# A transformer block on one core: last expert tiles planned in three segments, first keys ahead of other heads, ranks set anew

## The chip, the cores and the metric

The kernel runs on one core of a Trainium2 chip. Its time is the device time of one execution in microseconds (us). Beside it there is one profiled execution, with its own time and its own span (from the first to the last instruction). Engines: PE (TensorE, matrix products), DVE (VectorE), ACT (ScalarE), POOL (GpSimd), SP (SyncE, which here only issues transfers).

## The reference, cut to what matters

x is 4 batches of 512 tokens with 256 channels. Four layers follow each other, each added to x after a layer norm:

```python
x = x + _L0_attn_a_ref(_layernorm(x, axis=-1), ...)   # causal attention, 16 heads of 16, 4 key groups
x = x + _L0_ffn_ref(_layernorm(x, axis=-1), ...)      # 8 experts, the best 2 per token, 256 -> 176 -> 256
x = x + _L0_attn_b_ref(_layernorm(x, axis=-1), ...)   # memory attention, 4 banks of memories
x = x + _L0_ffn_ref(_layernorm(x, axis=-1), ...)      # the same experts again
```

The expert layer is `silu(x Wg) * (x Wu)`, times Wd, weighted by the two router probabilities. It is float32; the first attention is float16 with float32 sums.

## The kernel before

**The order is planned.** Each piece of work is a step with an engine, a rank, an assumed time and the steps it needs (`Work.add`, L122). `Work.order` (L141) goes through them as a list scheduler: it takes the step that can start first by the assumed times, or one of lower rank on the same engine that can start within PATIENCE times the first one's time. `NUDGE` (L94) adds a number to the rank of a kind of step. The result is a fixed order for each engine, and each engine executes its steps in it; a wait stops all that stands behind. `after` means that the step before must have finished (with `lands`, its transfer has landed), `behind` only that it was issued. In the first microseconds PE is given "warm" products where it would be idle (`keep_warm`, L130).

**The head.** SP issues x of batch 0 in two halves, the constants (`first_pack`), then the rest of x and the late constants (`load_late`). Then come the norm, the transposes (`f_turn`), q, k and v, and for the keys and queries the cosines, sines, mean square, `inv_rms`, `rotate`, in two parts p: 0 holds the queries of the first four heads and all keys, 1 the other heads. `first_keysT` and `place_keys` put group 0's keys into `kbd`, ACT two copies and DVE two (L1224, L1462). Scores run in 11 units per group and batch: `first` gives the maxima (PE L1002, DVE L1477), `second` the probabilities (PE L1025, ACT L1303), then `values`.

**Experts.** A token's normalised row is scattered twice (POOL, L1861) into a region of `xs` per expert. Within an expert the rows lie in the order batch, tile, token. 39 tiles of 128 rows (`TILES`) are worked through per layer: `load` (SP L903, 8 buffers), `xT` (PE L1119), `gate_up` (PE L1138, ACT L1347, DVE L1685 and L1689), `hidden` (PE L1147), `down` (PE L1155, DVE L1698 into `yo`, POOL L1876 scatters the rows into `ys`, 4 buffers). Which tile belongs to which expert and where its rows start is worked out by DVE (`plan`, L1575 to 1663) in three stages: 9 tiles as soon as 2 batches are routed, 8 with the third, 22 with the last. In the last stage there are SEGS = 16 segments, first what is left of each expert's full or mixed tiles of batches 0 to 2, then each expert's tiles that need batch 3. So tiles below MIXED = 31 hold all rows of the first three batches. Before the last stage SP writes zero rows behind each expert's rows (`pads`, L884), then it loads.

**Memory attention.** Per batch: `mq`, `den` (PE L1165, L1176), and per tile of 128 tokens `main` (PE L1184, DVE L1724, POOL L1883), `combT` (PE L1193: the sum of two banks' halves, transposed), `mem_out` (PE L1201, DVE L1740).

**The end.** `combine` (L455): for a batch of the second expert layer SP fetches `ys` in two halves of two transfers each (`fetch`, L913), DVE adds them to x (`join`, L1734 and L1735), SP stores each half (`store`, L919). Batches 0 to 2 wait for tile 30, batch 3 for tile 38. There are two fetch buffers in `kbd`, so a fetch waits for the join two batches before it.

## Time and profile before

| | before |
|---|---|
| median of 3 runs | 534.54 us (533.55 to 538.16) |
| the profiled execution | 532.43 us |
| its span | 530.6 us |
| granted clock over the span | 0.979 |
| PE busy | 480.4 us (91%) |
| DVE, ACT, POOL busy | 374.0 (70%), 269.3 (51%), 248.3 (47%) |
| HBM read and written | 28.89 and 25.00 MB |

How to read it: busy time counts an engine's instructions; matrix products are pipelined and their ends are modelled, so PE at 91% is not PE at its peak. The granted clock is a share of TensorE's 2.4 GHz; 0.50 is its lower level. A row of the timeline gives the start, the time, the engine, the line, the operation with what it writes and reads, and in square brackets how long the engine had been idle before and what released it. SPq and POOLq are issuing times of transfers. In the chain that ended last, each piece is what released the next.

### The profile page before, as it was taken

Reading aid. Unit: us, or ns where it says so; the run is one execution under the profiler, and the core shown is the slowest. Engines: PE = TensorE matmul, PEld = TensorE weight load, DVE = VectorE, ACT = ScalarE, POOL = GpSimd, SP = SyncE. Lnnn points to the kernel's source line nnn. Section 1 sums busy time; section 2 is a strip of 40 time slices with the busy share of each in tenths; the row PEclk is TensorE's granted clock in tenths of the full one; section 3 lists DMA queues with packets and bytes.
Section 4 is the critical chain, followed back from the end, with each engine's and each line's share of the span. In section 5 each row is a group of like instructions: output and inputs, shape, how many; then the busy total and the mean of one; then the engine's idle time right before and its main releaser. Section 6 shows DMA issues by size and latency. Waiting matters only on the chain.

```text
span 530.6 us, 10938 instructions
## 1 busy us (share of the span) xinstructions
PE 480.4 (91%) x3364; PEld 326.9 (62%) x3364; DVE 374.0 (70%) x1098; ACT 269.3 (51%) x642; POOL 248.3 (47%) x308
## 2 busy tenths in 40 slices
PE   7798999999999999899999979999979998999960
PEld 3445655765765676676676646675747765677740
DVE  5999989889999866754445557867878675344563
ACT  4587898887887874333333416514133533343310
POOL 5419339238650162473424654446464746333330
PEclk9899999999999999999999999999999989999995
DMA  8363800111230432374335492112141446433485
GB/s 276 129 261 142 178 19 10 53 58 45 62 101 2 121 111 71 115 196 136 105 101 168 81 179 40 41 40 81 40 141 60 149 132 181 130 100 117 148 279 182
DMA packets 43736, 60.77 MB, mean 115 GB/s; under 512 B 5856, under 2 KB 38240, under 8 KB 43040
## 3 DMA queue, kind: packets, MB, share of 16 engines
q1 hardware_dynamic: 33696, 38.24, 24.0%
q0 software_dynamic: 9984, 21.83, 13.9%
q8 instruction: 29, 0.48, 0.4%
q14 instruction: 27, 0.22, 0.1%
HBM read 28.89 MB, written 25.00 MB: 102 GB/s over the span
## 4 chain that ended last, share of the span: by engine, by line
PE 53%; DVE 12%; issue 5%; DMA 5%; POOL 4%; ACT 3%; SPq 1%; POOLq 0%; DVEq 0%; ACTq 0%
PE PS L1138 13%; PE PS L1155 9%; PE PS L1025 4%; PE PS L1184 3%; PE PS L1002 3%; POOL xs L1861 3%; PE PS L1119 2%; PE PS L1087 2%; PE PS L1147 2%; DMA ys<-yo,xin 2%; PE PS L1193 2%; DVE smax L1477 2%; PE PS L1201 2%; DMA kbd<-ys 2%; PE PS L1076 2%
## 5 line engine op out<-in xcount | busy, mean ns | idle before, releaser
L1876 POOL DMA_INDIRECT ys<-yo,xin x78 | 75.3, 966 | 106.2 <-DVE yo L1698 96.9
L1138 PE MATMUL PS<-wexp,xTt 128*128 x312 | 106.1, 467 | 2.7 <-issue 1.6
L1477 DVE TENSOR_REDUCE smax<-PS 128x1 f32<-128x512 f32 (+3 forms) x176 | 102.3, 634 | 6.6 <-PE PS L1004 6.1
L1303 ACT ACTIVATE prob<-PS 128x512 f16<-128x512 f32 (+1 forms) x176 | 92.7, 562 | 20.5 <-PE PS L1027 19.2
L1861 POOL DMA_INDIRECT xs<-xn,pos x64 | 62.5, 976 | 58.8 <-DVE pos L1572 41.7
L1155 PE MATMUL PS<-wexp,hT 88*128 x312 | 81.2, 387 | 2.3 <-ACT hT L1353 2.1
L1138 PEld LDWEIGHTS PS<-wexp,xTt 128*128 128x128 f32 x312 | 55.4, 191 | 25.3 <-issue 5.5
L1347 ACT ACTIVATE th<-PS 128x176 f32<-128x176 f32 x78 | 24.7, 317 | 84.0 <-PE PS L1138 84.0
L1685 DVE SCALAR_TENSOR_TENSOR sg<-th,PS 128x176 f32<-128x176 f32 x78 | 26.2, 336 | 58.2 <-ACT th L1347 57.9
L1155 PEld LDWEIGHTS PS<-wexp,hT 88*128 88x128 f32 x312 | 55.8, 191 | 15.2 <-issue 4.2
L1025 PE MATMUL PS<-qT,kbd 128*128 128x512 f16 (+3 forms) x256 | 60.8, 299 | 2.3 <-ACT qT L1295 1.0
L1002 PE MATMUL PS<-kbd,qT 128*128 128x512 f16 (+1 forms) x176 | 59.1, 360 | 2.7 <-DVE smax L1477 1.7
L1698 DVE TENSOR_SCALAR yo<-PS,xin 128x256 f32<-128x256 f32 x78 | 37.4, 482 | 27.8 <-PE PS L1155 22.1
L1353 ACT ACTIVATE hT<-PS 88x256 f32<-88x256 f32 x78 | 29.6, 379 | 41.4 <-PE PS L1147 40.4
L1027 PE MATMUL PS<-ident_b,mask_b 128*128 128x128 bf16 (+2 forms) x176 | 42.7, 243 | 0.0
L1004 PE MATMUL PS<-mask_b,ident_b 128*128 128x128 bf16 (+2 forms) x176 | 42.7, 243 | 0.0
L1043 PEld LDWEIGHTS PS<-vaug,prob 128*128 128x128 f16 x640 | 32.8, 96 | 16.0 <-ACT prob L1303 2.7
L1043 PE MATMUL PS<-vaug,prob 128*128 128x17 f16 x640 | 38.5, 171 | 1.5 <-ACT prob L1303 1.3
L1184 PE MATMUL PS<-late_rows,qT 128*128 128x512 f32 x64 | 32.2, 604 | 5.1 <-DVE qa L1724 4.7
L1147 PE MATMUL PS<-first_rows,hf 128*88 128x128 f32 x156 | 30.2, 275 | 4.8 <-DVE hf L1689 4.5
L1883 POOL TENSOR_TENSOR qa<-qa 128x256 f32<-128x256 f32 x32 | 23.2, 756 | 22.7 <-DVE qa L1724 22.6
L1025 PEld LDWEIGHTS PS<-qT,kbd 128*128 128x128 f16 x256 | 21.4, 98 | 15.8 <-ACT prob L1303 3.6
(210 smaller groups left out, 842.3 us busy)
## 6 DMA issues: line engine op xcount, KB each, us to landing
xin<-xs SPq DMA_DIRECT2D x78, 129.0 KB, 2.1
kbd<-ys SPq DMA_DIRECT2D x20, 256.0 KB, 4.1
wexp<-in_experts SPq DMA_DIRECT2D x4, 1216.0 KB, 9.2
xs<-zeros SPq DMA_DIRECT2D x32, 129.0 KB, 4.0
xn<-xn SPq DMA_DIRECT2D x8, 512.0 KB, 3.3
xall<-ys POOLq DMA_DIRECT2D x6, 512.0 KB, 7.2
out<-xall SPq DMA_DIRECT2D x8, 256.0 KB, 2.7
kbd<-kT SPq DMA_DIRECT2D x60, 32.0 KB, 2.2
```

Source lines behind the costliest of these rows:

```text
L1002: pe.matmul(o, qT1[:, b % 2, g, i * P:(i + 1) * P], kbd[:, g, r0:r0 + nr, 0:w], start=True, stop=False, skip_group_check=True)
L1004: pe.matmul(o[:, :, i * P:w], ident_b[:], mask_b[:].unsqueeze(1).to_broadcast([P, nr, P]), start=False, stop=True, skip_group_check=True). ...
L1025: pe.matmul(o[:, k], kbd[:, g, r0 + k, j * P:(j + 1) * P], qT2[:, g % 2, j * P:S], start=(k == 0), stop=False, skip_group_check=True)
L1027: pe.matmul(o[:, :, 0:P], mask_b[:], ident_b[:].unsqueeze(1).to_broadcast([P, nr, P]), start=False, stop=True, skip_group_check=True).then ...
L1043: mm = pe.matmul(o[:, i, r0 + k], prob[:, u % NPR, k * w + (i - j) * P:k * w + (i - j + 1) * P], vaug[:, b, j, g], start=(n == 0 and k == ...
L1138: mm = pe.matmul(PS[:, bank, 0:2 * FI], xTt[:, j % NXT, kc * P:(kc + 1) * P], wexp[:, bass.ds(expert[f, j], 1), kc * 2 * FI:(kc + 1) * 2 * FI]
L1155: mm = pe.matmul(PS[:, bank, 0:D], hT[:, j % 2, c * P:(c + 1) * P], wexp[0:FH, bass.ds(expert[f, j], 1), DOWN + c * D:DOWN + (c + 1) * D] ...
L1184: pe.matmul(PS[:, bank], sig[:, b % 2, kc, i * P:(i + 1) * P], late["mem"][:, kc], start=True, stop=True).then_inc(filled[bank], 1)
L1303: act.activation(prob[:, u % NPR, 0:nr * w], PS[:, bank, 0:nr * w], ACT.Exp, scale=ATT_SCALE)\
L1477: dve.tensor_reduce(smax[:, i, REP * g + r0:REP * g + r0 + nr], PS[:, bank, 0:nr * w].rearrange("p (r w) -> p r w", r=nr), AX.X, ALU.max). ...
L1861: pool.indirect_dma_start(xs[f], bass.IndirectOffsetOnAxis(pos[:, f, b, i, k:k + 1], axis=0), xn[:, b % 2, i, k], None).then_inc(scattered ...
L1876: pool.indirect_dma_start(ys[f], bass.IndirectOffsetOnAxis(xin[:, j % NXIN, D + 1:D + 2].bitcast(I32), axis=0), yo[:, j % NYO], None).then ...
```

## The change

- **Three parts.** SEGS is 24. In the last stage, batch 3's tiles are in two parts: what its first 256 tokens need, then the rest. Tiles below MIXED_HALF = 35 hold all rows of that first half, and `fetch` of half 0 of batch 3 waits for tiles 31 to 34. In the planner the second half's fetch stands `behind` the first one's, no longer `after` it. `count` on PE gives a second set of counts (5 small products more). DVE's final plan works on 24 segments; the mask and the table `upto` are bfloat16, and the table is made by DVE in `bank_shift` (two operations) in place of being loaded.
- **First keys.** DVE's cosines and mean square of the other heads stand behind its `place_keys`, and that behind the first queries. ACT places one copy of the keys, DVE three.
- **Loads and presets.** SP waits for the constants before it issues `load_late`. The memset of `kbd` is four of a quarter each.
- **combT** is a transpose and a product that adds to it, in place of two products.
- **The planner:** NUDGE is new throughout, PATIENCE is 0.13 for 0.022, some assumed times differ, and after 10 us the warm products stand closer (0.16 for 0.25) until 24.

The diff, cut to its core (of NUDGE, the first lines):

```diff
 MIXED = 2 * (B - 1) * S // P + NE - 1
-SEGS = 2 * NE
+MIXED_HALF = (2 * (B - 1) * S + S) // P + NE - 1
+SEGS = 3 * NE
 PLAN_N = [-(-(hi - lo) // 4) * 4 for _, lo, hi in STAGES]
...
-NUDGE = {("apply", 0): 4.5, ("bank_shift",): -3, ("combT", 2): 0.5, ("combT", 3): -18, ("cosines", 1): 12,
...
-         ("xT", 0): 54, ("xT", 1): 1}
+NUDGE = {("bank_shift",): 3, ("banks",): 17, ("combT", 1): 19, ("combT", 2): -21, ("count", 0): -17,
+         ("den", 2): 7, ("f_stats", 2): -31, ("first", 0): 16, ("first", 1): 25, ("first", 3): 2,
+         ("gate_up", 0): 2, ("gate_up", 1): 2, ("hidden", 0): -10, ("inv_rms", 1): 14, ("join", 1): 73,
+         ("load_x", 0): 11, ("main", 0): -2, ("main", 1): -10, ("main", 2): 37, ("main", 3): -9,
...
-    WARM_FROM, WARM_UNTIL, WARM_GAP, WARM_STEP = 3.2, 25.0, 0.4, 0.25
-    HOP, PATIENCE = 0.05, 0.022
+    WARM_FROM, WARM_RISE, WARM_UNTIL, WARM_GAP, WARM_STEP = 3.2, 10.0, 24.0, 0.4, (0.25, 0.16)
...
-def tiles_with(b):
-    return MIXED if b < B - 1 else TILES
+def tiles_with(b, h=1):
+    return MIXED if b < B - 1 else TILES if h else MIXED_HALF
...
     for p in range(2):
+        ahead = [(DVE, "place_keys")] if b == 0 and p else []
         last = [(p0, "queries", b - 1, p)] if b else []
         w.add(POOL, r(), (1.75, 2.05)[p], "sines", b, p, after=made + [(POOL, "constants")] + last)
-        w.add(e, r(), ((0.75, 0.95), (1.3, 1.75))[b > 0][p], "cosines", b, p, after=made + [(POOL, "constants")] + last)
+        w.add(e, r(), ((0.75, 0.95), (1.3, 1.75))[b > 0][p], "cosines", b, p, after=made + [(POOL, "constants")] + last, behind=ahead)
         w.add(ACTE, r(), (0.53, 0.75)[p], "square", b, p, after=made + [(p0, "mean_square", b - 1, p)] * (b > 0))
-        w.add(e, r(), ((0.85, 1.1), (2.2, 2.7))[b > 0][p], "mean_square", b, p, after=[(ACTE, "square", b, p)])
+        w.add(e, r(), ((0.85, 1.1), (2.2, 2.7))[b > 0][p], "mean_square", b, p, after=[(ACTE, "square", b, p)], behind=ahead)
         w.add(ACTE, r(), 0.45, "inv_rms", b, p, after=[(e, "mean_square", b, p)] + last)
         w.add(e, r(), ((0.65, 0.92), (1.55, 2.1))[b > 0][p], "rotate", b, p, after=[(POOL, "sines", b, p), (e, "cosines", b, p)])
...
-                for a in (ACTE, DVE):
-                    w.add(a, r(), 1.0, "place_keys", after=[(PE, "keysT" if a == ACTE else "first_keysT", *[b] * (a == ACTE)),
-                                                            (POOL, "presets")])
+                place_rank = r()
+                w.add(ACTE, place_rank, 0.5, "place_keys", after=[(PE, "keysT", b), (POOL, "presets")])
         w.add(e, r(), ((0.38, 0.95), (0.6, 1.75))[b > 0][p], "queries", b, p, after=[(ACTE, "inv_rms", b, p), (e, "rotate", b, p),
               (e, "keys", b), (DVE, "presets")] + old + [(e, "queries", b, 0)] * p)
         if p == 0:
             w.add(ACTE, r(), 0.5, "keysT", b, after=[(PE, "keysT", b)] + [(ACTE, "place_keys")] * (b == 0)
                   + [(SP, "place_keys", b - 2, g) for g in range(b == 2, NG) if b >= 2])
+            if b == 0:
+                w.add(DVE, place_rank, 1.27, "place_keys", after=[(PE, "first_keysT"), (POOL, "presets")],
+                      behind=[(DVE, "queries", 0, 0)])
             for g in range(b == 0, NG):
                 w.add(SP, r(), 2.4, "place_keys", b, g, after=[(ACTE, "keysT", b), (POOL, "presets")] + [(PE, "second", b - 1, g, NU - 1)] * (b > 0),
...
-    w.add(PE, rank, 0.1, "count", f, n, after=[(DVE, "choose", f, b) for b in range(STAGES[n][0])], banks=banks,
+    w.add(PE, rank, 0.3 if n == LAST else 0.1, "count", f, n, after=[(DVE, "choose", f, b) for b in range(STAGES[n][0])], banks=banks,
           emptied=(DVE, "plan", f, n, 3 if n == 1 else 0))
-    prior = [(DVE, "plan", f, n - 1, 3)] if n else [(DVE, "down", f - 1, TILES - 1)] if f else [(DVE, "presets")]
-    for part, time in enumerate((1.67, 1.9 if n == LAST else 1.3, 1.1 if n == LAST else 0.85, 1.5)[:4 - (n == LAST)]):
+    prior = [(DVE, "plan", f, n - 1, 3)] if n else [(DVE, "down", f - 1, TILES - 1)] if f else [(DVE, "bank_shift")]
+    for part, time in enumerate((2.9 if n == LAST else 1.67, 2.9 if n == LAST else 1.3, 1.6 if n == LAST else 0.85, 1.5)[:4 - (n == LAST)]):
         w.add(DVE, rank, time, "plan", f, n, part, after=[(DVE, "plan", f, n, part - 1)] if part else
               [(PE, "count", f, n)] + prior)
...
-    done = tiles_with(b)
-    rows = [(POOL, "down", f, j) for j in range(done - NYO, done)]
+    rows = [[(POOL, "down", f, j) for j in range(tiles_with(b, h) - NYO, tiles_with(b, h))] for h in range(2)]
     n = JOINED.index((f, b)) if (f, b) in JOINED else None
     for k in range(2):
         if n is None:
-            w.add(POOL, rank + 0.1 * k, 1.4, "add", f, b, k, after=rows + [(POOL, "add", f, b, 0)] * k,
+            w.add(POOL, rank + 0.1 * k, 1.4, "add", f, b, k, after=rows[1] + [(POOL, "add", f, b, 0)] * k,
                   behind=[(POOL, "pow", 1, 0)], lands=8.0)
         else:
-            w.add(SP, rank + 0.1 * k, 0.75, "fetch", f, b, k, after=rows + ([(DVE, "join", *JOINED[n - 2], 1)] if n >= 2 else [])
-                  + [(SP, "fetch", f, b, 0)] * k, lands=3.3)
+            w.add(SP, rank + 0.1 * k, 0.75, "fetch", f, b, k, after=rows[k] + ([(DVE, "join", *JOINED[n - 2], 1)] if n >= 2 else []),
+                  behind=[(SP, "fetch", f, b, 0)] * k, lands=3.3)
     for h in range(2 * (n is not None)):
...
                   behind=prior(DVE))
             w.add(POOL, times[i], 0.7, "main", b, i, kc, after=[(DVE, "main", b, i, kc)], behind=prior(POOL))
...
-        w.add(PE, times[i + 1], 0.89, "combT", b, i, after=[(POOL, "main", b, i, kc) for kc in range(KC)], banks=(3, 4),
+        w.add(PE, times[i + 1], 0.66, "combT", b, i, after=[(POOL, "main", b, i, kc) for kc in range(KC)], banks=(3, 4),
...
     w.add(SP, -998, 0.5, "load_x", 1, behind=[(SP, "load_x", 0)], lands=2.8)
-    w.add(SP, -997, 0.5, "constants", behind=[(SP, "load_x", 1)], lands=6.3)
-    w.add(SP, -996, 4.0, "load_late", behind=[(SP, "constants")], lands=11.0)
+    w.add(SP, -997, 0.5, "constants", behind=[(SP, "load_x", 1)], lands=5.0)
+    w.add(SP, -996, 4.0, "load_late", after=[(SP, "constants")], lands=10.0)
     w.add(SP, unit(2), 2.0, "load_experts", behind=[(SP, "place_keys", 0, NG - 1)], lands=20.0)
...
+        pl_mask = sb("pl_mask", [P, JL, SEGS], BF16)
+        upto = sb("upto", [P, SEGS, SEGS], BF16)
         pl_prod = sb("pl_prod", [P, JL, SEGS])
         pl_base = sb("pl_base", [P, JL])
...
                     elif kind == "load_late":
+                        sp.wait_ge(first_loaded, 16)
...
                     elif kind == "fetch":
                         f, b, h = a
-                        for j in range(tiles_with(b) - NYO, tiles_with(b)):
+                        for j in range(tiles_with(b, h) - NYO, tiles_with(b, h)):
                             wait_for_row(sp, f, j)
                         n = JOINED.index((f, b))
                         if n >= 2:
...
                                            stop=(c == batches - 1))
+                        if batches == B:
+                            for c in range(B - 1):
+                                pe.matmul(PS[:, bank, NE:2 * NE], ones_b[:], part[:, c], start=(c == 0), stop=False)
+                            for i in range(NT // 2):
+                                mm = pe.matmul(PS[:, bank, NE:2 * NE], ones_b[:], chosen[:, B - 1, i], start=False,
+                                               stop=(i == NT // 2 - 1))
                         mm.then_inc(filled[bank], 1)
...
                             u = KC * (NT * b + i) + kc
-                            for n in range(2):
-                                mm = pe.matmul(PS[:, bank, kc * P:(kc + 1) * P], scl[:, u % 4, n], ident_f,
-                                               start=(n == 0), stop=(n == 1))
+                            o = PS[:, bank, kc * P:(kc + 1) * P]
+                            pe.transpose(o, scl[:, u % 4, 0], ident_f)
+                            mm = pe.matmul(o, scl[:, u % 4, 1], ident_f, start=False, stop=True, skip_group_check=True)
...
                         act.wait_ge(kbd_cleared, 1)
-                        for r in range(REP // 2):
-                            act.activation(kbd[r * QROW:(r + 1) * QROW, 0, r], bank16(bank)[0:QROW, 0:S], ACT.Copy)\
-                               .then_inc(keys_placed[0], 32)
+                        act.activation(kbd[0:QROW, 0, 0], bank16(bank)[0:QROW, 0:S], ACT.Copy)\
+                           .then_inc(keys_placed[0], 16 * REP)
...
                         dve.wait_ge(kbd_cleared, 1)
-                        for r in range(REP // 2, REP):
+                        for r in range(1, REP):
...
-                            link(dve.tensor_tensor(pl_cmp[:], count.unsqueeze(2).to_broadcast([P, NE, 16]), steps,
+                            counts = PS[:, bank, 0:2 * NE].rearrange("p (k e) -> p k e", k=2)
+                            more = pl_mask[:, 0:16].rearrange("p a b -> p (a b)")[:, 0:2 * NE * 16]\
+                                .rearrange("p (k e s) -> p k e s", k=2, e=NE)
+                            link(dve.tensor_tensor(more, counts.unsqueeze(3).to_broadcast([P, 2, NE, 16]),
+                                                   late["steps"].unsqueeze(1).unsqueeze(1).to_broadcast([P, 2, NE, 16]),
                                                    ALU.is_gt))
-                            dve.tensor_reduce(pl_tmp[:], pl_cmp[:], AX.X, ALU.add).then_inc(taken[bank], 1)
+                            dve.tensor_reduce(pl_need[:], more, AX.X, ALU.add).then_inc(taken[bank], 1)
                             out_of(dve, "count", f, n)
-                            dve.tensor_tensor(pl_tiles[:, NE:], pl_tmp[:], pl_all[:], ALU.subtract)
-                            link(dve.scalar_tensor_tensor(pl_hi[:, NE:], pl_tmp[:], float(P), late["base"],
+                            dve.tensor_tensor(pl_tiles[:, NE:2 * NE], pl_need[:, 1], pl_all[:], ALU.subtract)
+                            dve.tensor_tensor(pl_tiles[:, 2 * NE:], pl_need[:, 0], pl_need[:, 1], ALU.subtract)
+                            dve.scalar_tensor_tensor(pl_hi[:, 2 * NE:], pl_need[:, 0], float(P), late["base"],
+                                                     ALU.mult, ALU.add)
+                            dve.scalar_tensor_tensor(pl_hi[:, NE:2 * NE], pl_need[:, 1], float(P), late["base"],
+                                                     ALU.mult, ALU.add)
+                            link(dve.scalar_tensor_tensor(pl_lo[:, 2 * NE:SEGS], pl_need[:, 1], float(P), late["base"],
                                                           ALU.mult, ALU.add))
                             dve.tensor_tensor(pl_skip[:, NE:], pl_lo[:, NE + 1:], pl_hi[:, NE:], ALU.subtract)
                         if piece == 0:
-                            link(dve.tensor_tensor(pl_sum[:, 0:segs, 0:segs], own.unsqueeze(1)
-                                                   .to_broadcast([P, segs, segs]), late["upto"][:, 0:segs, 0:segs],
+                            link(dve.tensor_tensor(sums, own.unsqueeze(1)
+                                                   .to_broadcast([P, segs, segs]), upto[:, 0:segs, 0:segs],
                                                    ALU.mult))
-                            link(dve.tensor_reduce(pl_upto[:, 0:segs], pl_sum[:, 0:segs, 0:segs], AX.X, ALU.add))
+                            link(dve.tensor_reduce(pl_upto[:, 0:segs], sums, AX.X, ALU.add))
                         elif piece == 1:
                             link(dve.tensor_tensor(mask, pl_upto[:, 0:segs].unsqueeze(1).to_broadcast([P, tiles, segs]),
...
                         dve.wait_ge(late_loaded, 16)
+                        own, other = late["tiles"][:, 0:SEGS].unsqueeze(2), late["tiles"][:, 0:SEGS].unsqueeze(1)
+                        link(dve.tensor_tensor(upto[:], other.to_broadcast([P, SEGS, SEGS]),
+                                               own.to_broadcast([P, SEGS, SEGS]), ALU.is_le))
+                        link(dve.tensor_scalar(upto[:], upto[:], float(P), None, ALU.mult))
                         link(dve.tensor_reduce(bmax[:], late["bank"].rearrange("p k n h -> p k h n"), AX.X, ALU.max))
...
                         pool.memset(vaug[:], 1.0).then_inc(presets, 1)
-                        pool.memset(kbd[:].bitcast(U32), 0).then_inc(kbd_cleared, 1)
+                        for g in range(NG):
+                            ins = pool.memset(kbd[:, g].bitcast(U32), 0)
+                        ins.then_inc(kbd_cleared, 1)
```

## Rows read from the trace of the kernel before

**Rows 1.** Busy time in stretches; span, busy us (instructions) of PE, PEld, DVE, ACT, POOL; clock, DMA, GB/s.
```profile
24.00:60.00 36.00, 32.00 (x318) 18.50 (x316) 35.31 (x84) 28.31 (x62) 19.03 (x30) 1.00 0.53 187
60.00:180.00 120.00, 115.87 (x1314) 76.94 (x1313) 109.33 (x298) 98.48 (x207) 54.25 (x78) 1.00 0.18 52
300.00:400.00 100.00, 91.40 (x460) 60.91 (x458) 71.02 (x208) 37.56 (x77) 54.53 (x63) 1.00 0.37 85
500.00:515.00 15.00, 12.61 (x55) 8.32 (x54) 10.82 (x24) 4.07 (x13) 4.36 (x6) 1.00 0.85 282
24.00:515.00 491.00, 463.01 (x3271) 317.86 (x3268) 351.68 (x1050) 257.86 (x617) 233.83 (x280) 1.00 0.37 106
```

**Rows 2.** The same view, the head as a whole and short stretches around the lower clock.
```profile
13.00:24.00 11.00, 8.14 (x53) 4.89 (x53) 9.99 (x21) 5.70 (x14) 5.38 (x8) 0.85 0.38 157
...
22.00:24.00 2.00, 2.00 (x17) 1.62 (x16) 1.93 (x8) 1.07 (x2) 0.00 (x0) 0.50 0.12 31
...
428.00:430.00 2.00, 2.00 (x5) 1.28 (x4) 0.98 (x5) 0.00 (x0) 0.63 (x1) 0.50 0.31 84
```

**Rows 3.** Timeline of the head: start, us, engine, line, operation [idle before].
```profile
4.64 1.38 DVE L1386 TENSOR_SCALAR f_veps<-f_mv 128x2 f32<-128x2 f32 x1
7.30 1.09 ACT L1237 ACTIVATE xh<-xall,f_nb,f_rstd 128x256 f16<-128x256 f32 x2 [0.23 <-DVE f_nb L1417]
8.95 0.23 DVE L1395 CAST ident_h<-first_rows 128x128 f16<-128x128 f32 x1 [1.04 <-DMA first_rows<-in_first_pack]
...
18.00 0.95 DVE L1444 TENSOR_REDUCE ms<-sq 128x48 f32<-128x768 f32 x1
18.69 0.28 POOL L1844 CAST before_b<-late_rows 128x128 bf16<-128x128 f32 x1
19.09 0.42 DVE L1454 TENSOR_TENSOR ka<-rota,inv 128x256 f16<-128x256 f32 x1
20.41 0.85 DVE L1462 COPY kbd<-PS 32x512 f16<-32x512 f16 x2
24.08 0.38 PE L1002 MATMUL PS<-kbd,qT 128*128 128x512 f16 x1
```

**Rows 4.** The chain that ended last: a combT, then six transposes.
```profile
401.26 0.89 PE PS L1193 x8
402.15 0.66 PE PS L1119 x6
```

**Rows 5.** The final plans: timeline of the first; SP's waits in the second.
```profile
221.29 0.42 DVE L1608 TENSOR_TENSOR pl_sum<-pl_tiles,late_rows 128x256 f32<-128x256 f32 x1
223.02 0.55 DVE L1613 TENSOR_TENSOR pl_mask<-pl_upto,late_rows 128x384 f32<-128x384 f32 x1
225.77 0.42 PE L1147 MATMUL PS<-first_rows,hf 128*88 128x128 f32 x2 [2.05 <-DVE hf L1689]
...
SPq L836 <- DVE plan L1631: 7.2, 1, 7.2
SPq L895 <- DMA xs<-zeros: 1.7, 1, 1.7
```

**Rows 6.** The tail: two transfers from the chain, the others from the timeline.
```profile
499.80 5.80 DMA kbd<-ys
...
508.34 0.96 POOL L1876 DMA_INDIRECT ys<-yo,xin  x1 [5.96 <-DVE yo L1698]
512.01 0.96 POOL L1876 DMA_INDIRECT ys<-yo,xin  x1 [2.71 <-DVE yo L1698]
...
515.80 4.07 DMA ys<-yo,xin
...
523.50 0.69 DVE L1734 TENSOR_TENSOR xall<-xall,kbd 128x512 f32<-128x512 f32 x1 [3.13 <-DMA kbd<-ys]
526.15 0.69 DVE L1734 TENSOR_TENSOR xall<-xall,kbd 128x512 f32<-128x512 f32 x1 [1.24 <-DMA kbd<-ys]
```

**Rows 7.** Timeline of PE in memory attention: its longest wait there.
```profile
387.43 1.98 PE L1184 MATMUL PS<-late_rows,qT 128*128 128x512 f32 x4 [3.03 <-DVE qa L1724]
```

29 lines of the change are left out of this document (13 added, 16 removed).

## Prediction, made before the change was run

> **What bounds the kernel now.** I read the busy time by stretch first, because the page's totals mix four kinds of work [rows 1]. TensorE (PE) is the engine that everything else hangs on from 24 us to 514.5 us: busy 32.0 of 36 us, then 115.9 of 120, 91.4 of 100 in the memory-attention stretch, and 12.6 of 15 at the end of its work. A matmul removed there should come back almost whole; a matmul that only starts earlier helps only if the others follow. VectorE (DVE) is the second bound: 9.99 of 11 us before 24 us [rows 2] and 35.3 of 36 between 24 and 60. So in the first 60 us both are nearly full, and DVE more than PE.
>
> Then three places in order of time. The head [rows 2, 3], where the constants arrive and the first keys are made; the two final plans of the expert tiles [rows 5]; and the tail [rows 6], read in the chain that ended last and in the timeline. In the tail PE has stopped, and what counts is one row of waits: the last scatter of the experts' results lands 4.07 us after its issue, two halves are fetched, joined by DVE and stored.
>
> My sum is made on the profiled execution, 532.43 us (its span is 530.6, so 1.8 us lie around it). The median of the three runs is 534.54, 2.1 us above it; I take the same difference off the median.
>
> **Part 1: the tail.** Before, both halves of batch 3 are fetched after the last tile. That tile's scatter lands at 515.80 + 4.07 = 519.87. The first half is joined from 523.50, 3.6 us later; the second is issued behind it and behind a store, and joined from 526.15 [rows 6]. With three parts, the first half needs only tiles up to 34, so it can be fetched, joined and stored while tiles 35 to 38 are computed. Behind the last scatter one half remains, and its join can start where the first one starts now: 526.15 - 523.50 = 2.65 us less. The join of 1.4 us and the last store stay. At least 1.5 us of it should come, as behind the last scatter it is then no longer queued behind another half and a store; at most 3.5, if the scatter lands sooner without fetches beside it. I take 2.65.
>
> Ahead of it, DVE has joins in its fixed order in front of tile work. One join waits for a fetch that took 5.80 us; the next product (L1685) comes only after it, and POOL, which needs 0.96 us for a scatter, sits idle for 5.96 us [rows 6]. PE loses 2.4 us in 500 to 515, of which 0.5 is after its last matmul [rows 1]. The joins' rank moves 73 later, behind all tiles. But the planner places a step as soon as it believes it can start, and it believes that a fetch lands in 3.3 us; the edit of `behind` for `after` even lets it believe the second half comes sooner. So I take half of the 2 us: 1.0, with the range from 2.3 gained to 2.5 lost.
>
> **Part 2: combT.** 16 steps of eight matmul records, 0.89 us each on the chain, 0.111 per record. A transpose is one record (0.66 us for six, the same 0.11), a float32 product two [rows 4]. Each step goes from 8 to 6 records: 2 x 0.111 x 16 = 3.55 us of PE. The stretch has 8.6 us of idle PE per 100 [rows 1], part of it DVE's (3.03 us at 387 [rows 7]), which shorter products only lengthen. I take 3.0, bounds 1.5 and 3.55.
>
> PE's clock fell to half twice: 0.50 in 22 to 24 us, after PE had lain idle, and 0.50 in 428 to 430, where the chain has router products and transposes ahead of it and PE has no pause by the record [rows 2]. There 2 us passed for 1 us of work at full clock. The Trainium skill (TensorE: Matmul & The Clock Gate, PE-mode transpose) says that a transpose does not count as busy for the clock as a product does. It speaks against this edit, and the fall before 430 agrees with it; by it the sum would lose what the rival below prices, without it the 3.0 us stand. I keep 3.0, since 300 to 400 ran at 1.00 with all its transposes [rows 1].
>
> **Part 3: the head.** The constants land at 8.95 us, and the ident cast and ACT's weights wait for them, while ACT's last normalised tile ends at 7.30 + 1.09 = 8.39 [rows 3]. With the late loads held back until the constants are there, they can land at least 0.56 us earlier in effect; the memset of kbd in four pieces may also free the statistics (a 128x2 operation took 1.38 us beside it). I take 0.6, bounds 0 and 1.2. The late loads then start only when the constants have landed. Their first user in the head is a POOL cast at 18.69 [rows 3], for the router far behind; out_weights and the bank steps follow the first scores. I cost that at nothing; a statistics step of batch 1 that waits for its x would cost DVE what it waits.
>
> The first keys: DVE does the mean square of the other heads at 18.00 for 1.1 us just ahead of the keys at 19.09, and the first score starts only at 24.08, behind all queries [rows 3]. Moving these behind the keys, with the cosines of the other heads also, can bring the first score some 3.5 us forward. But DVE's work is not less, it is only in another order, and DVE is full to 60 us: what comes back is only what it can push beyond 60, where it is busy 109 of 120 us [rows 1]. I take 1.5, bounds 0 and 3.5.
>
> DVE gets more work: one more copy of the keys, 0.42 (two took 0.85), and the `upto` table, two operations on 576 elements. Two rows at 256 and 384 elements, 0.42 and 0.55 [rows 5], give 0.001 us per element, so 0.75 each: 1.9 us in all against ACT's one copy less. Half of it shows: 0.9 lost, bounds 0 and 1.9. The denser warm products fill a PE that was busy 8.14 of 11 us there and at the lower clock at 22 us [rows 2], and may keep its clock: nothing, or 0.5 us either way.
>
> **Part 4: three segments in the final plans.** 24 instead of 16 segments. Table and sum: 2 operations from 256 to 576 elements, +0.33 each. Mask, two products and two sums: 5 from 384 to 576, +0.19 each. The counts: 2 at +0.13, and three more small ones, about 0.3. Together 0.66 + 0.96 + 0.26 + 0.3 = 2.2 us per final plan, and there are two. Storing the mask in two bytes saves nothing that a row shows. In the first, DVE runs the plan piece from 223.02 on ahead of the next product, and PE stands 2.05 us for it [rows 5]; the two pieces before that product grow by 0.33 + 0.33 + 0.56 + 0.58 = 1.8, and some tile work may be put between. I take 1.2. In the second, SP waits for the plan (7.2 us) and then for its own zero rows (1.7 us) [rows 5]: the loads of the last 22 tiles start later by up to 2.2, but PE has tiles in hand. I take 0.4. The counting products add 0.1 each. Together 1.8 lost, bounds 0.5 and 4.4.
>
> **Part 5: the order.** All ranks and the patience (0.022 to 0.13) are changed, so every engine's order may differ at every place. The largest PE waits left (3.03 at 387, 2.05 at 225 [rows 5, 7]) are of the kind that an order makes or removes. PE's idle time from 24 to 515 is 491.0 - 463.0 = 28.0 us in all [rows 1]. From 5 gained to 5 lost; I take 0.5 gained.
>
> **The sum.** -2.65 - 1.0 - 3.0 - 0.6 - 1.5 + 0.9 + 1.8 - 0.5 = -6.55. 532.43 - 6.55 = 525.9 for a profiled run like the one before; 534.54 - 6.55 = 528.0 for the median. Likely range of this case: 523.5 to 531.
>
> **Rivals.**
> *The order gains more* (0.17). The waits at 387, 225 and most of the joins' go: 3.0 + 2.0 + 1.0 beyond the sum, 522.0. For it: they are single waits with one cause each. Against it: the planner's costs did not see them before.
> *Only the tail is real* (0.22). DVE holds the head and memory attention: combT gives 1.5, the head 0, the plans cost 2.5, the joins nothing. -2.65 - 1.5 + 2.5 = -1.65: 532.9. For it: 35.3 of 36 us of DVE.
> *A join stands in front of the last tiles* (0.12, the other side). If the join of batch 3's first half is in DVE's order ahead of tile 35's results, DVE waits until tile 34 is stored (508.34 + 4.1), fetched (3.6 as now) and joined (1.4), 517.4; with 0.7 for the output POOL issues tile 35's scatter at 518.1, where it is 512.01 now [rows 6]. Everything behind shifts by 6.1 us or more: 528.0 + 1.0 + 6.1 = 535.1, and up to 543 if earlier joins wait too. It decides once that join precedes the output of tile 35; behind tile 38's it costs nothing. Against it: the nudge of 73.
> *The clock falls in memory attention* (0.07). Once per batch for some 3.4 us, as before 430, half of it lost: 4 x 1.7 = 6.8 back, 534.8. The Trainium skill's page named above would expect this of combT's transposes.
> *The split does nothing* (part of the second): SP reaches the early fetch only behind the last store, and then 2.65 is missing too: 535.5.
>
> **Chances.** Forecast 0.42, the others 0.17, 0.22, 0.12, 0.07. Within 1% is 529.2 to 539.9, about what a measurement of this kernel can tell. Faster: 0.36 of the forecast's 0.42, all 0.17 of the order's, and 0.02 of the tail-only case: 0.55. Slower: two thirds of the joins' case, those where an earlier join waits too, 0.08. Same: the rest, 0.37. The range for 8 in 10 reaches through the tail-only rival and the clock's, and leaves out the joins' case and the lower end of the order's: 521.0 to 535.0.
>
> **What would show it.** Step 1: one pair of fetches behind the last scatter, not two, and a join ending about 5 us after the scatter lands. Joins: POOL's idle time before tile 34's scatter below 3 us. Step 2: 96 records on the combT line and its two in place of 128, and PE busy 3.5 us less in that stretch. Step 3: the keys before 17.9 us, the first score before 21.5. Step 4: masks of 576 elements near 0.75 us; a PE wait above 3 us in the first final plan. I am wrong if the first score comes early and 60 us holds no more finished work than before, if a join waits over 3 us while PE has tiles, or if the granted clock is below 0.97 over the span.

## The result, and the profile after

The changed kernel takes 539.45 us (median of 18 executions, 537.47 to 542.71), the kernel before 536.41 (18 executions, 531.22 to 540.05): ratio 1.0077, 95% interval 1.0055 to 1.0098. It is 0.8% slower, and not 1.2% faster. The time lies outside the range of 521 to 535. Its profiled execution took 539.17 us, with a span of 537.4; that is 6.8 us over the span shown of before (530.6). The medians are 3.0 us apart, so less than half of these 6.8 us is the change; the rest is that the execution shown of before was one of its fastest (532.43 against a median of 536.41).

The page and the busy time by stretch of the changed kernel (columns as in [rows 1]):

```profile
span 537.4 us, 10922 instructions
...
PEclk9979999999999999999999999999979999999976
...
24.00:60.00 36.00, 29.37 (x266) 15.50 (x266) 34.73 (x82) 25.05 (x56) 19.03 (x30) 0.91 0.72 212
60.00:180.00 120.00, 118.44 (x1365) 79.24 (x1364) 111.30 (x293) 102.60 (x214) 54.15 (x78) 1.00 0.13 40
300.00:400.00 100.00, 89.17 (x423) 58.97 (x422) 70.87 (x206) 36.39 (x76) 55.05 (x63) 0.97 0.35 80
460.00:500.00 40.00, 39.30 (x186) 28.75 (x185) 17.40 (x47) 14.86 (x47) 14.91 (x16) 1.00 0.34 100
500.00:515.00 15.00, 11.50 (x52) 8.32 (x51) 7.63 (x18) 3.92 (x12) 4.26 (x5) 0.96 0.74 246
```

Against [rows 1], PE has 266 products instead of 318 between 24 and 60 us, at a mean granted clock of 0.91 instead of 1.00; it is nearly full until 180; and it is less busy in memory attention (89.2 for 91.4) and in the tail (11.5 for 12.6). The clock stood at its lower level in four places where PE was still at work:

```profile
28.00:36.00 8.00, 6.65 (x27) 2.54 (x27) 7.76 (x24) 3.61 (x7) 0.87 (x2) 0.57 0.84 311
186.00:190.00 4.00, 4.00 (x19) 2.25 (x18) 2.62 (x20) 3.65 (x8) 0.00 (x0) 0.57 0.53 136
390.00:398.00 8.00, 3.47 (x11) 2.86 (x12) 2.25 (x8) 1.12 (x3) 7.14 (x10) 0.57 0.38 111
513.00:520.00 7.00, 6.08 (x16) 4.32 (x17) 2.27 (x5) 1.46 (x4) 1.15 (x1) 0.55 0.81 267
```

By the trace's record of the clock these are 6.8, 3.4, 6.8 and 6.8 us at 0.50. The kernel before had two such stretches of 3.4 us while PE worked [rows 2]. Three of the four stand in or right behind a PE wait that the new order made; in the 10 us ahead of the one at 186.0 PE has no wait above 0.5 us. The 18 executions of the changed kernel have a mean granted clock of 0.9694, and 26 of the kernel before on another such chip 0.9757. By the slope in the last section that difference is worth 2.6 us, an estimate across two chips, and so most of the 3.0 us.

**The head.** Timeline of the changed kernel (start, us, engine, line, operation, [idle before]):

```profile
16.98 1.02 DVE L1466 TENSOR_TENSOR ka<-rota,inv 128x256 f16<-128x256 f32 x1
18.83 1.27 DVE L1474 COPY kbd<-PS 32x512 f16<-32x512 f16 x3 [0.49 <-PE PS L982]
20.31 0.38 PE L1008 MATMUL PS<-kbd,qT 128*128 128x512 f16 x1
...
20.13 0.96 DVE L1451 TENSOR_TENSOR rota<-qk,rope 128x768 f32<-128x768 f16 x1
21.12 0.95 DVE L1456 TENSOR_REDUCE ms<-sq 128x48 f32<-128x768 f32 x1
23.20 0.69 DVE L1489 TENSOR_REDUCE smax<-PS 128x1 f32<-128x512 f32 x1
25.27 0.74 DVE L1393 BATCH_NORM_STATS2 f_stat<-xall 128x6 f32<-128x256 f32 x2
26.40 0.74 DVE L1393 BATCH_NORM_STATS2 f_stat<-xall 128x6 f32<-128x256 f32 x2
28.28 0.34 PE L1008 MATMUL PS<-kbd,qT 128*128 128x384 f16 x1 [2.41 <-DVE smax L1489]
```

The keys stand at 16.98 (19.09 in [rows 3]) and the first score starts at 20.31 (24.08). But the reduction that empties its PSUM bank comes only at 23.20, behind the copies, cosines and mean square of the other heads, and the statistics of batch 1 stand behind the second reduction. PE waits 2.41 us, and the half clock follows.

**Memory attention.** PE and POOL around the loss at 390 us, same view:

```profile
388.70 1.13 PE L1197 MATMUL PS<-late_rows,qT 128*128 128x512 f32 x2 [0.96 <-DVE qa L1752]
391.62 0.96 POOL L1891 DMA_INDIRECT xs<-xn,pos  x1 [0.30 <-issue]
392.59 2.77 POOL L1913 TENSOR_TENSOR qa<-qa 128x256 f32<-128x256 f32 x4
394.06 0.48 PE L1206 MATMUL PS<-first_rows,qa 128*128 128x128 f32 x1 [4.23 <-POOL qa L1913]
```

The scatter at 391.62 is the last of eight that POOL does in one block, 382.7 to 392.6. combT of the last batch needs POOL's step, which stands behind them all, so PE waits 4.23 us, where it waited 3.03 in [rows 7].

**The tail.** First the chain that ended last (start, us, what), then the timeline:

```profile
508.13 5.74 DMA xin<-xs
...
524.50 4.71 DMA ys<-yo,xin
529.34 0.37 SPq L919
529.70 0.04 issue
529.75 3.12 DMA kbd<-ys
```

```profile
499.47 0.96 POOL L1906 DMA_INDIRECT ys<-yo,xin  x1 [2.82 <-DVE yo L1726]
...
503.78 4.13 SPq L919 DMA_DIRECT2D kbd<-ys  x8
508.13 0.42 SPq L909 DMA_DIRECT2D xin<-xs  x1
513.92 0.69 PE L1132 MATMUL PS<-first_rows,xin 128*128 128x128 f32 x2 [3.50 <-DMA xin<-xs]
517.11 1.15 POOL L1906 DMA_INDIRECT ys<-yo,xin  x1 [6.34 <-DVE yo L1726]
529.34 0.89 SPq L919 DMA_DIRECT2D kbd<-ys  x2
532.89 0.69 DVE L1762 TENSOR_TENSOR xall<-xall,kbd 128x512 f32<-128x512 f32 x1 [2.60 <-DMA kbd<-ys]
```

The load of the last tile (L909) stands behind eight fetch transfers of 256 KB each. By the code all nine wait for the same scatter, that of tile 30 (issued at 499.47), and SP goes on at 503.78. The load is issued at 508.13 and lands 5.74 us later (median over all loads: 2.2), PE waits 3.50 us for it, and POOL issues the scatter of tile 35, whose last product stands behind this wait in PE's order, only after 6.34 us of idleness. Behind the last scatter there is one pair of fetches, as the split was to bring.

For all comparisons below I use three stretches that can be read in any of the timelines: the **memory stretch**, from the first gate/up product of the last tile of the first pass to the last output addition of memory attention; the **tail stretch**, from the first gate/up product of tile 28 of the second pass to the end; and of that the part **behind the last scatter** (from the end of its instruction on POOL). These traces give:

```
kernel                memory stretch      tail stretch        behind last scatter
before                107.0               48.6                13.9
before_again          107.6               48.3                14.1
combT_alone, _b       108.0, 106.4        49.3, 48.2          14.2, 14.4
load_late             107.2               49.9                12.7
edits_old_order x3    106.5, 109.1, 110.2 47.1, 47.3, 47.2    13.5, 13.6, 12.7
products_first        106.2               48.1                13.5
best                  106.5               48.8                11.9
order_alone, _b       108.6, 108.3        49.7, 48.1          13.1, 12.6
changed, _again       104.9, 106.1        51.5, 49.1          11.7, 11.3
late_half             106.2               50.8                13.1
stats_behind          104.9               51.5                11.2
load_first x3         104.8, 106.2, 106.2 46.8, 46.6, 46.4    12.8, 12.5, 12.7
scatter_split         103.6               46.6                13.0
```

The 6.8 us between the two profiled executions divide so: the first tile of the first pass starts 3.5 us later (187.6 for 184.1), the memory stretch is 2.1 shorter, the tail stretch 2.9 longer, and the tile passes between take 2.5 more in sum. The forecast, term by term, had -1.2, -3.0, -3.65 and +1.3 for these four, so the tail is the largest miss (6.5 us), then the start of the first tile (4.7), the passes (1.2) and the memory stretch (0.9). Each is read from one execution of either kernel.

### The profile page after: what moved, and what is told of

Same layout as the page of the kernel before. It is cut to its first block, busy times and chain, and to the rows that moved or that the text cites. A ratio compares the mean times of both kernels' runs of the same rounds, so it can differ in the third digit from the quotient of the medians.

```text
span 537.4 us, 10922 instructions
## 1 busy us (share of the span) xinstructions
PE 484.5 (90%) x3353; PEld 329.2 (61%) x3353; DVE 380.0 (71%) x1107; ACT 268.5 (50%) x641; POOL 248.5 (46%) x311
## 3 DMA queue, kind: packets, MB, share of 16 engines
q0 software_dynamic: 9984, 21.83, 13.6%
## 4 chain that ended last, share of the span: by engine, by line
PE 54%; DVE 15%; POOL 4%; issue 4%; DMA 4%; ACT 2%; SPq 1%; POOLq 0%; DVEq 0%; ACTq 0%
PE PS L1151 15%; PE PS L1168 10%; PE PS L1031 4%; DVE smax L1489 3%; PE PS L1160 3%; POOL xs L1891 3%; PE PS L1008 3%; PE PS L1093 3%; PE PS L1132 2%; DMA ys<-yo,xin 2%; PE PS L1178 2%; PE PS L1082 2%; PE PS L1214 1%; PE PS L1197 1%; PE PS L1033 1%
## 5 line engine op out<-in xcount | busy, mean ns | idle before, releaser
L1906 POOL DMA_INDIRECT ys<-yo,xin x78 | 75.8, 972 | 107.6 <-DVE yo L1726 98.0
L1151 PE MATMUL PS<-wexp,xTt 128*128 x312 | 109.1, 474 | 2.3 <-issue 1.8
L1315 ACT ACTIVATE prob<-PS 128x512 f16<-128x512 f32 (+1 forms) x176 | 91.3, 561 | 18.4 <-PE PS L1033 17.0
L1008 PE MATMUL PS<-kbd,qT 128*128 128x512 f16 (+1 forms) x176 | 61.2, 368 | 4.9 <-DVE smax L1489 4.5
L1031 PE MATMUL PS<-qT,kbd 128*128 128x512 f16 (+3 forms) x256 | 62.3, 301 | 0.7 <-ACT prob L1315 0.6
L1353 ACT ACTIVATE xTt<-PS 128x256 f32<-128x256 f32 x78 | 27.7, 381 | 19.6 <-PE PS L1132 19.5
```

The lines of the kernel that those rows point to most:

```text
L1008: pe.matmul(o, qT1[:, b % 2, g, i * P:(i + 1) * P], kbd[:, g, r0:r0 + nr, 0:w], start=True, stop=False, skip_group_check=True)
L1031: pe.matmul(o[:, k], kbd[:, g, r0 + k, j * P:(j + 1) * P], qT2[:, g % 2, j * P:S], start=(k == 0), stop=False, skip_group_check=True)
L1151: mm = pe.matmul(PS[:, bank, 0:2 * FI], xTt[:, j % NXT, kc * P:(kc + 1) * P], wexp[:, bass.ds(expert[f, j], 1), kc * 2 * FI:(kc + 1) * 2 * FI]
L1315: act.activation(prob[:, u % NPR, 0:nr * w], PS[:, bank, 0:nr * w], ACT.Exp, scale=ATT_SCALE)\
L1906: pool.indirect_dma_start(ys[f], bass.IndirectOffsetOnAxis(xin[:, j % NXIN, D + 1:D + 2].bitcast(I32), axis=0), yo[:, j % NYO], None).then ...
```

## Experiments

Letters name the theories; what each says stands in the quoted expectation that names it. The runs went to several chips. Only the four with the kernel before near 533 us (before_again, scatter_split, products_first, combT_alone_b) ran on one like that of the result. On the others it took 577 to 581 us, because the engines stood still at about ten places (below, under the unexpected); there a ratio says something of the order of steps and of those stops together, and single stretches of the trace say more.

### The load of the last tile

The first pair of kernels takes the suspected cause away from the changed kernel and puts it into the kernel before:

```
 ORDER, PLACE = plan_work().order()
+ORDER[SP].remove(("load", 1, TILES - 1))                                     # load_first
+ORDER[SP].insert(ORDER[SP].index(("fetch", 1, 0, 0)), ("load", 1, TILES - 1))
```
```
+for step in (("fetch", 1, 1, 1), ("fetch", 1, 0, 1)):                        # load_late
+    ORDER[SP].remove(step)
+    ORDER[SP].insert(ORDER[SP].index(("load", 1, TILES - 1)), step)
```

> The changed kernel with one step of SP's order moved: the load of the last tile (38) stands ahead of the four pairs of fetches of batches 0 and 1 of the second pass, instead of behind them. Nothing else differs. Theory T (the load behind 2 MB of fetches starves the tail: POOL 6.3 us idle, PE 3.5 us, and PE at half clock for 8 us behind it): the tail lost 4.4 us more than the kernel before (lag 4.3 at 490 us, 8.7 at the last scatter), and half of the clock's loss can stay, so 3.5 to 5.0 us below the changed kernel's 539.45: 534.5 to 536, ratio to before 0.991 to 0.999. PE's wait for the load of tile 38 below 1 us, and the granted clock in 512 to 520 above 0.9. Rival H (what was lost, was lost by 60 us and is only carried through; the tail's waits are as long with any order): within 1 us of 539.45, ratio 1.005 to 1.010.

> The kernel before with the suspected cause put in: SP's load of the last tile stands behind both halves of batches 0 and 1 (eight transfers) instead of behind two halves (four). Theory T: the load lands some 3 us later, PE waits for it and its clock falls as in the changed kernel, so slower by 3 to 5 us, ratio 1.005 to 1.010. Rival H: the load is early enough all the same, or what it costs is given back by the earlier joins: within 1 us, ratio 0.998 to 1.002.

> The same program as load_first, once more, because in that run every engine stood still with its work ready for 2 to 6 us at about ten places, which neither trace shown so far has. Where those stops are missing (time of the kernel before near 536, not 578): theory T (the last tile's load behind 2 MB of fetches is the tail's loss) gives 534.5 to 536, ratio 0.991 to 0.999, a PE wait for the load of tile 38 below 1 us; rival H (lost by 60 us and carried through) ratio 1.005 to 1.010. Where they are there again, no bound for either, and a ratio of 1.019 as in the first run would say that the load's place feeds them.

> The changed kernel with the last tile's load ahead of the four pairs of fetches, now beside the changed kernel itself. Theory T: 3.5 to 5 us below it (its ratio to before lower by 0.006 to 0.009), on any chip, since the wait stands in the tail. Rival H: the two within 0.002 of each other.

Measured: load_first 1.0192 (1.0143 to 1.0241), 1.0158 (1.0118 to 1.0198) and 1.0110 (1.0030 to 1.0190); load_late 0.9998 (0.9969 to 1.0027). Beside load_first_c, the changed kernel itself:

> The changed kernel itself, so that the runs beside it have it on the same chip. On a chip like that of the first comparison: ratio 1.0055 to 1.0098. On the chip of the last two calls: by theory O (the order of steps is what loses) between load_first (1.016 to 1.019) and late_half (1.029), near 1.02 to 1.025; by rival E (the edits lose) near edits_old_order, 1.000 to 1.006.

It had 1.0146 (1.0078 to 1.0213). The intervals are too wide to show 4 us, so the ratios decide nothing for the changed kernel. The place does: in load_first (timelines of SP and PE)

```profile
540.19 8.01 SPq L911 DMA_DIRECT2D xin<-xs  x3
548.38 4.22 SPq L921 DMA_DIRECT2D kbd<-ys  x8
557.57 0.42 PE L1162 MATMUL PS<-first_rows,hf 128*88 128x128 f32 x2 [0.52 <-DVE hf L1719]
```

the load goes first, PE's longest wait from 544 to 560 us is 0.52 us, and the tail stretch takes 46.4 to 46.8 us in three traces, where the changed kernel's takes 49.1 and 51.5. So theory T holds at its place, with 2.3 to 5.1 us. Its mirror was a near miss: load_late did lengthen tiles 28 to 38, by 2.1 us (30.3 for 28.2 in combT_alone on the same chip), but with the joins done earlier the end came 1.5 us sooner, and the tail stretch grew by 0.6 only. PE waits for the load here too, with 3.4 us at half clock from 555.2:

```profile
555.29 0.69 PE L1122 MATMUL PS<-first_rows,xin 128*128 128x128 f32 x2 [1.59 <-DMA xin<-xs]
```

So a late load costs in both orders, 2.1 us here and more where the wait is 3.5 us, and in this one the earlier fetches paid for most of it. Where the load was early enough, moving it further ahead gained nothing:

```
(all edits in the old order) + the two lines of load_first                   # best
```

> All edits of the changed kernel in the order of the kernel before, and the load of the last tile ahead of the fetches of batches 0 and 1. Theories O and T together: 4 to 7 us below the kernel before, ratio 0.987 to 0.993. Rival E: 0.998 to 1.004. If only theory T holds of the two, it lies 1.5 to 2.5 us below edits_old_order, since only two pairs of fetches stood ahead of the load there.

best had 1.0051 (1.0020 to 1.0083), its tail stretch 48.8 against 47.1 to 47.3 of edits_old_order. In best two pairs of joins stand in front of a tile's work on DVE, the second waits 1.24 us for its fetch, PE waits 0.99 us behind them at 556.1, and 3.4 us at half clock follow from 558.0. The same step that gains 2.3 us or more in one order loses about 1.6 in another.

### Edits and order apart

edits_old_order is the changed kernel's text with the kernel before's ranks, costs and patience in the planner; order_alone is the reverse.

> All edits of the program text in the changed kernel (three parts in the final plans, the fetch of a half that waits for 35 tiles, the transpose in combT, the tables made on the chip, the held-back late loads, the memset in four pieces), but in the kernel before's order of steps: its ranks, costs and patience. Theory O (the new order is the loss, the edits are worth what their places show): combT -3.0, the split half -2.65, plans and tables +1.8 to +2.7: 3 to 4 us below the kernel before, ratio 0.992 to 0.995. Rival E (the edits themselves cost: the final plans and the DVE work of the head are worth more than 5 us): ratio 1.000 to 1.008.

> The same program as edits_old_order, once more, for the same reason. Theory O (the new order is the loss, the edits are worth what their places show: combT -3.0, the split half -2.65, plans and tables +1.8 to +2.7): ratio 0.992 to 0.996 where the stops are missing. Rival E (the edits cost more than they give): 1.000 to 1.008.

> edits_old_order on a chip without the stops, if it is one (kernel before near 533). The traces since have put numbers to the edits in the old order: combT nothing at the end (ratio 1.0029 alone), the first final plan +2.2, the head +1, the split half -0.6 to -2. By these the edits cost 1 to 4 us in sum: ratio 1.002 to 1.007, near products_first (1.0073). Theory O as first stated (edits worth 3.9) would need 0.992 to 0.996.

> The program text of the kernel before (two parts in the final plans, both halves fetched behind the last tile, combT with two products) in the changed kernel's order of steps. Theory O: the order alone costs what the changed kernel lost and what its edits gave, 3.0 + 3.9 = about 7 us, ratio 1.010 to 1.015; the load of the last tile lands some 5 us late here too. Rival E: the order costs at most 2 us, ratio 0.997 to 1.004.

> order_alone on the same chip. If the losses of the changed order (PE wait behind POOL's scatters with the half clock behind it, the last tile's load, 0.09 us more per tile of the second pass, the head) add up as read, 5 to 9 us and without the 2.5 us that the transposes give in this order: ratio 1.010 to 1.018. If the order is worth nothing by itself and the edits are the loss: 0.997 to 1.004.

Measured: edits_old_order 1.0005 (0.9968 to 1.0042), 1.0029 (0.9996 to 1.0061) and 0.9964 (0.9926 to 1.0002); order_alone 1.0257 (1.0212 to 1.0301) and 1.0268 (1.0227 to 1.0308). All on chips with the stops. On such chips the new order alone costs and the edits alone do not. The sizes of theory O do not stand: the edits gave nothing that can be measured instead of 3.9 us, and 15 us for the order is far more than order and edits together cost on the result's chip (3.0). Neither kernel was measured on a chip without the stops. The nearest there is products_first (below), all edits in the old order with four steps moved, and it cost 1.0073, as much as the changed kernel. So how the 3.0 us of the result divide between edits and order is not shown. In order_alone the load of the last tile is waited for as well, 1.79 and 2.41 us.

### combT alone

```
-for n in range(2):
-    mm = pe.matmul(PS[...], scl[:, u % 4, n], ident_f, start=(n == 0), stop=(n == 1))
+pe.transpose(o, scl[:, u % 4, 0], ident_f)
+mm = pe.matmul(o, scl[:, u % 4, 1], ident_f, start=False, stop=True, skip_group_check=True)
```

> The kernel before with one edit: of combT's two products the first is a transpose, so 96 records instead of 128 in the memory attention; order and planner's costs as before. Theory P (PE bounds that stretch): 3.0 us less, 1.5 to 3.55, ratio 0.993 to 0.997, PE busy 3.5 us less from 300 to 430. Rival C (PE's clock pays for the transposes, or DVE and POOL bound the stretch): within 0.8 us of before or slower, ratio 0.9985 or more; C by the clock would show a granted clock below 0.95 somewhere between 300 and 430, C by DVE a clock of 1.00 and as much more idle PE as there is less busy.

> combT_alone once more. Theory W: the PE wait is 3.4 us again, 0.4 longer than with two products, and a stretch at half clock of 3.4 or 6.8 us follows; the memory attention takes 106 to 109 us where it took 107.0 to 107.2 with two products, ratio 0.995 to 1.000. Rival P (PE gets its 3.0 us back, the first run's stretches at half clock were chance): 103.5 to 104.5 us, ratio 0.993 to 0.996.

> The kernel before, for its profile on this chip. Its memory attention (from the first product of the last tile of the first pass to the last output of that stage) should take 107.0 to 107.2 us as in the two traces with its text and order, with the PE wait of 3.0 us and, by theory W (the clock falls when that wait reaches 3.4 us, not for the transposes' own sake), no stretch at half clock behind it. From tile 28 of the second pass to the end: 48.6 to 49.3.

Measured: 0.9968 (0.9935 to 1.0002) on a chip with the stops, 1.0029 (0.9996 to 1.0061) on the other. The 3.0 us did not come. PE at its longest wait in memory attention, first before_again, then combT_alone_b:

```profile
388.69 3.63 PE L1184 MATMUL PS<-late_rows,qT 128*128 128x512 f32 x4 [3.02 <-DVE qa L1724]
```
```profile
389.14 2.96 PE L1184 MATMUL PS<-late_rows,qT 128*128 128x512 f32 x4 [3.37 <-DVE qa L1724]
```

The wait ends when DVE and POOL get there, and shorter products before it make it longer. Of the half clock, theory W is refuted: before_again, with two products per combT and a wait of 3.02, fell to 0.50 at 388.6 for 3.4 us, where the execution shown of before, with the same wait, did not. So whether the clock falls behind a wait of this length changes from execution to execution; with the 4.2 us of the changed order all nine traces of it show 6.8 us at half. The 12 executions of combT_alone_b had a mean granted clock of 0.9712, the 26 of the kernel before beside them 0.9757, and by the before kernel's own slope (last section) that is 1.9 us, more than its whole lag of 1.6 in the mean. Why its clock was lower is not settled.

### The split half

```
 ORDER, PLACE = plan_work().order()
+MIXED_HALF = TILES                                                           # late_half
```

> The changed kernel with one number changed: the first half of the last batch waits for all 39 tiles again instead of 35. Order and all else as in the changed kernel. If the split is worth what its place shows, two pairs of fetches stand behind the last scatter again and the end moves back by 2.65 us (2.0 to 3.5): ratio to the kernel before 1.012 to 1.014, where the changed kernel has 1.0077. If the early fetch only takes DMA time from the last loads and gives nothing at the end: 1.005 to 1.009.

Measured: 1.0293 (1.0257 to 1.0330), 0.0147 above changed_again on another such chip. These are 8.5 us, most of which its place does not explain. At its place: behind the last scatter 13.1 us instead of 11.3 and 11.7. So the split gives 1.4 to 1.8 us in the changed order. The last scatter, first in late_half, then in changed_again (chain: start, us from issue to landing; the changed kernel's took 4.71, shown above), tells why it is not more:

```profile
576.37 2.40 DMA ys<-yo,xin
```
```profile
570.11 4.45 DMA ys<-yo,xin
```

From its landing to the end late_half takes 11.7 us and the other two take 8.0 and 8.2, which is 3.5 to 3.6 less. But the first half's fetch now runs beside that scatter (issued at 524.29 in the changed kernel, landed by 528.8), and the scatter takes 2.1 to 2.3 us more to land. It is the same wherever it can be read: 2.59 to 2.66 us in order_alone, order_alone_b and load_late, where no fetch was issued in the 4 us before the scatter, and 4.04 to 5.86 in stats_behind, the three of load_first and scatter_split, where one was issued within 1 us of it. In the kernel before it was 4.07, beside a fetch issued 2.5 us earlier that landed at 518.9. In the old order the split gives 0.3 to 1.7 (12.7 to 13.6 for 13.9 to 14.4 with two halves left). I had expected 2.65. In load_first, with the last scatter earlier, the part is 12.5 to 12.8 again: that scatter takes 5.34 to 5.53 us to land there.

### The head

```
+for step in (("f_stats", 1, 1), ("f_stats", 1, 0)):                          # stats_behind
+    ORDER[DVE].remove(step)
+    ORDER[DVE].insert(ORDER[DVE].index(("first", 0, 0, 5)) + 1, step)
+for step, behind in ((("f_scale", 1), 7), (("bank_shift",), 8)):
+    ORDER[DVE].remove(step)
+    ORDER[DVE].insert(ORDER[DVE].index(("first", 0, 0, behind)) + 1, step)
```

> The changed kernel with DVE's order altered in one place of the head: the two statistics of batch 1 (2.3 us) stand behind the sixth score reduction instead of behind the second, their scaling behind the eighth, the table of the final plans (1.05 us) with the bank step behind the ninth. Theory D (DVE's other work between the first reductions let PE run dry at 26 to 28 us, and half clock from 29.0 to 35.8 followed): no PE wait over 1 us between 24 and 30, no fall of the clock there, 5.9 us less lag at 40 us than the changed kernel's 6.5, of which the later stretches keep a part: 0.5 to 2 us at the end, its ratio lower by 0.001 to 0.004. Rival A (the lag of the head is made up before the attention ends whatever it was): clock restored, end within 0.001.

Measured: 1.0260 (1.0213 to 1.0307), slower than changed_again. The wait at 28 us went, and came back as a longer one, in PE's timeline of stats_behind:

```profile
26.63 0.34 PE L1014 MATMUL PS<-kbd,qT 128*128 128x384 f16 x1 [0.21 <-DVE smax L1495]
33.31 0.91 PE L958 MATMUL PS<-ident_h,xh 128*128 128x128 f16 x7 [5.25 <-issue]
```

PE's own fixed order has batch 1's transposes behind the ninth score; they need the statistics that I had moved, and 5.25 us of idleness and 6.8 at half clock from 31.8 us took the place of 2.41 and 6.8. So the experiment decides nothing on theory D; it shows that this engine's order can't be mended without PE's. What the head costs at the end stays open.

### The wait in memory attention

```
 (load_first)                                                                 # scatter_split
+for k, behind in enumerate(((2, 0), (1, 1))):
+    ORDER[POOL].remove(("main", B - 1, 0, k))
+    ORDER[POOL].insert(ORDER[POOL].index(("scatter", 1, 1, *behind)) + 1, ("main", B - 1, 0, k))
```
```
 (edits_old_order)                                                            # products_first
+for k in (0, 1):
+    ORDER[DVE].remove(("main", B - 1, 0, k))
+    ORDER[DVE].insert(ORDER[DVE].index(("wgt", B - 1)) + 1 + k, ("main", B - 1, 0, k))
+for k, behind in enumerate(((1, 1), (3, 1))):
+    ORDER[POOL].remove(("main", B - 1, 0, k))
+    ORDER[POOL].insert(ORDER[POOL].index(("scatter", 1, 1, *behind)) + (k == 0), ("main", B - 1, 0, k))
```

> load_first with one more change of order: on POOL, the first two steps of memory attention of the last batch stand inside the block of eight scatters of batch 1 (behind the third and the sixth) instead of behind all eight (10.2 us). Theory S (that block, which the changed order puts right where PE needs POOL, is the loss of 5.9 us between 390 and 400 us): PE's wait of 4.2 us there falls below 1.5, no half clock follows (now 6.8 us), and the memory attention takes 99 to 102 us instead of 104.8 to 106.2; at the end 2.5 to 5 us less than load_first, ratio to before 1.003 to 1.010 on this chip. Rival G (the time is bound by PE and DVE over the whole stretch, the wait only gathers it): the wait moves to another place, 104 us or more, ratio 1.010 to 1.019.

> edits_old_order with two changes of order at the PE wait of 3.4 us in memory attention: on DVE the first two weighting steps of the last batch stand ahead of the plan's last two pieces (2.2 us), and on POOL its first two steps stand behind the sixth and seventh of the eight scatters. Theory S: the wait falls below 1.5 us and no half clock follows it, the stretch takes 102 to 104.5 us instead of 106.5 to 109.1, ratio to before 0.993 to 0.999 on this chip, where edits_old_order has 1.0005 and 1.0029. Rival G: 106 us or more, ratio 1.000 to 1.005.

Measured, on the chip without stops: scatter_split 532.97 us, ratio 1.0015 (0.9986 to 1.0045); products_first 537.80 us, 1.0073 (1.0041 to 1.0105). The waits of PE in scatter_split, and its busy time where the changed kernel had 3.47 of 8 us at 0.57:

```profile
389.49 1.12 PE L1202 MATMUL PS<-late_rows,qT 128*128 128x512 f32 x2 [1.71 <-DVE qa L1757]
391.59 0.33 PE L1211 MATMUL PS<-first_rows,qa 128*128 128x128 f32 x1 [0.98 <-POOL qa L1918]
397.81 0.33 PE L1211 MATMUL PS<-first_rows,qa 128*128 128x128 f32 x1 [1.49 <-POOL qa L1918]
...
390.00:398.00 8.00, 4.56 (x22) 2.64 (x21) 4.93 (x13) 1.23 (x3) 7.25 (x9) 1.00 0.29 90
```

One wait of 4.23 became three of 1.7, 1.0 and 1.5: POOL is busy 7.25 of these 8 us, so the wait was spread and not removed, as rival G has it, though the stretch is shorter than G allows (104 us or more) and longer than theory S has it (99 to 102). What came back is the half clock and about 1.3 us (memory stretch 103.6 for 104.9). With the tail's 4.9 us, which the load's place gives, the profiled span falls from 537.4 to 531.1. The ratio falls from 1.0077 to 1.0015, which is 3.3 us, though the two were measured on different chips. So three moved steps, the load and the two on POOL, take back most of what the change lost, and what is left is no loss that can be measured, and no gain. What each of them is worth alone on such a chip was not measured.

products_first has the same pattern (waits of 1.2, 1.6 and 1.4, no half clock, memory stretch 106.2) and no gain at all: with the mean granted clock of the kernel before (0.9757 both) it is 4.5 us slower in the mean, above what rival G allowed too. Its trace, one of its fastest executions (534.00), shows 1.8 us of this, at the first final plan. PE's wait there, first before_again, then products_first:

```profile
225.10 0.66 PE L1147 MATMUL PS<-first_rows,hf 128*88 128x128 f32 x2 [2.03 <-DVE hf L1689]
```
```profile
227.99 0.42 PE L1171 MATMUL PS<-first_rows,hf 128*88 128x128 f32 x2 [3.79 <-DVE hf L1728]
```

This is the 1.8 us by which I had let the two plan pieces grow, all of it on PE. Where its other 2.7 us lie is open. No kernel that I ran is shown to be faster than the kernel before.

## Why the prediction failed, step by step

**Joins, -1.0: the step that failed most.** I looked at DVE's joins in front of tile work, and saw that the edit lets the planner believe that second halves come sooner. I asked what that does to DVE, and not what stands behind the fetches on SP's queue. There it was the load of the last tile. The tail stretch up to the end of the last scatter's instruction takes 39.8 us (37.8 in changed_again), where before it took 34.7 (34.2 in before_again): 3.1 to 5.6 us longer instead of 1.0 shorter. With the load in front it takes 33.7 to 34.1. What I had priced did come: POOL's idle time before tile 34's scatter is 2.72 us, as the sign that I had named (below 3, where it was 5.96). The term had left out the load of the last tile, whose wait the sum put at nothing.

**Split half, -2.65: right mechanism, mis-sized.** One pair of fetches stands behind the last scatter, and the last join ends 5.1 us after the scatter lands (529.21 to 534.3; I had written about 5). Worth 1.4 to 1.8. I had left a gain open "if the scatter lands sooner without fetches beside it"; the split puts a fetch beside it, and it lands later. The difference of two join starts in [rows 6] contained time in which SP issued a store and a second pair; the remaining half still waits for its own fetch of 3.12 us and a scatter that took 4.71 instead of 4.07.

**combT, -3.0: true for PE, true at the end only in one order.** The records are 96 for 128, and PE is busy 2.2 us less from 300 to 400 (I had said 3.5), although 6.8 us of that stretch ran at half clock. In the changed order the memory stretch is 108.3 to 108.6 with two products and 104.8 to 106.2 with the transpose: 2.1 to 3.8 us. In the old order it is 107.0 to 107.6 with two products and 108.0 and 106.4 with the transpose, and the whole kernel gains nothing that can be measured. I had named the wait at [rows 7] as one that shorter products lengthen, and had not drawn the conclusion that the gain ahead of it is lost in it. The Trainium skill (TensorE: Matmul & The Clock Gate, PE-mode transpose) had spoken against this edit. products_first and scatter_split have all the transposes, and their mean clocks of 0.9757 and 0.9749 are those of the kernel before beside them (0.9757); combT_alone_b had 0.9712. So no run here shows the transposes by themselves lowering the clock, and none excludes a small part.

**Head, -0.6 - 1.5 + 0.9: the signs came, the gain did not.** The keys stand at 16.98 (I had said before 17.9) and the first score at 20.31 (before 21.5). The constants are there at 7.87 instead of 8.95, but that is no sign of the held-back loads: combT_alone_b, without that edit, has them at 7.83 and before_again at 8.69. The first qkv product starts at 10.12 for 10.33, and at 9.99 in combT_alone_b. So of the 0.6 nothing is shown. I had priced the early score by what DVE could push beyond 60 us, at worst nothing. But a score product needs its reduction to free a bank: three start early, then PE waits for DVE, and half clock follows for 6.8 us. The first tile started 3.5 us later instead of 1.2 earlier. How much of that is the head is not shown: between 24 and 60 us it is 52 products behind, but by 170 us the two kernels have finished equally many (1520 since 24 us), and another half-clock stretch came at 186.0. So 60 us held less finished work than before, which I had named as a sign of being wrong, and the granted clock (0.968 in the profiled execution) is the other.

**Final plans, +1.8: right size, wrong place.** The operations on 576 elements took 0.75 us, as worked out:

```profile
223.64 0.34 DVE L1717 TENSOR_TENSOR hf<-sg,PS 128x176 f32<-128x176 f32 x1
223.89 0.75 DVE L1636 TENSOR_TENSOR pl_mask<-pl_upto,late_rows 128x576 bf16<-128x576 f32 x1
224.03 0.42 PE L1160 MATMUL PS<-first_rows,hf 128*88 128x128 f32 x2 [0.91 <-DVE hf L1717]
```

But the new order puts tile work between the pieces, and PE's wait there fell from 2.05 to 0.91; over the 14 us around it PE is as busy as before (11.49 and 11.48). In the old order the wait rose to 3.79. My test for this step, a PE wait above 3 us, was wrong for the changed kernel and right for the edits alone.

**Order, -0.5: taken as nearly free.** Besides the load and the head, the new order lengthened the wait behind POOL's scatters (4.23 for 3.03) and came with 6.8 us of half clock in all nine traces that have this wait, and in the steady tiles of the second pass PE is busy 39.3 of 40 us where it was busy 40.0: five tiles took 12.6 us before and four take 10.4 now, 0.09 us more for each. I had given it a range of 5 us to either side, and then left the slow side out of the forecast's own range.

**The rivals.** The result comes closest to the join's rival in its number (535.1 to 543), but its mechanism was another: no join stood in front of a tile, a tile's load stood behind the fetches. The rival of the clock had four more stretches of 3.4 us in memory attention. There are four in all, longer ones (23.9 us at half clock while PE works, where the kernel before had 6.8); one of them lies in memory attention, three stand beside a wait, and no run shows a transpose as a cause.

## To carry to other kernels

When an edit lets transfers be issued earlier, list what stands behind them on the same queue, and ask for the last load first; an order that is replanned can cost as much as the edits it was planned for can give, so test the edits in the old order and the order without the edits, on the chip of the result. A transfer taken out of the last wait may run beside the transfer that ends it: here it took back more than half of what the split gave. A gain on the busiest engine arrives only as far as the next wait that another engine ends: look for that wait before adding the gain to the sum. Waits of 2 to 4.2 us on TensorE often came with 3.4 to 6.8 us at half clock, and that of 4.2 us in memory attention did in all nine traces, so price a new wait with what comes with it.

## What the runs showed of the hardware, unexpected

**The clock goes with most of the scatter between executions.** Of 26 executions of the kernel before on one chip (29 were taken; 537.28, 538.16 and one of 2661.67 us are left out), the fastest took 529.22 us at a mean granted clock of 0.981 and the slowest 537.14 at 0.967; a line through all has a slope of 4.1 us per 0.01 of mean clock (correlation -0.87). A stretch of 3.4 us at half lowers the mean by 0.0032, so by this slope it costs about 1.3 us, an estimate. The stretches do not come at the same places in every execution: before_again has them at 20.0, 224.8, 313.5 and 388.6, the first profiled execution of the same kernel at 20.6 and 426.8.

**Some chips stop where others don't.** On three chips the kernel before took 577 to 581 us instead of 533 to 536. Single operations take the same time (a score's reduction, a scatter), but engines stand idle with their inputs ready, nearly each time during or just after a block of POOL's eight scatters. combT_alone, busy time, then timeline:

```profile
112.00:119.00 7.00, 6.61 (x77) 3.93 (x74) 3.58 (x9) 5.82 (x13) 5.07 (x5) 1.00 0.25 87
119.00:122.00 3.00, 0.00 (x0) 0.00 (x0) 0.59 (x2) 0.00 (x0) 2.11 (x3) 0.85 0.33 111
...
121.41 1.02 DVE L1477 TENSOR_REDUCE smax<-PS 128x1 f32<-128x384 f32 x2 [5.76 <-remote]
122.84 0.60 ACT L1303 ACTIVATE prob<-PS 128x512 f16<-128x512 f32 x1 [4.07 <-remote]
```

Only POOL goes on scattering. What releases the others the profile calls "remote", something it does not record; on the chip of the result DVE waited 1.42 us at the same place. What it is stays open. It makes a ratio of two orders on such a chip a measurement of the stops as well.

**A memset holds up a small operation beside it.** The first `f_veps` operation (128x2 on DVE) overlaps POOL's clearing of kbd. With the clearing in one piece, which ends at 6.00 us, it ends at 6.03 in six of seven traces and takes 1.26 to 1.50 us in all. With four pieces it takes 0.49 to 0.64 us in nine of thirteen traces and ends at 5.24 or 5.25, just behind the third piece (5.22), and 1.50 to 1.81 us in the other four (scatter_split, late_half, load_first_b, stats_behind), where it ends with the fourth piece or later (6.13 to 6.39). So four pieces helped in most executions and not in all.

**A two-byte operation.** Scaling the table in bf16 on DVE, a tensor_scalar on 576 elements, took 0.31 us, a tensor_tensor on as many with float32 0.75. The Trainium skill (VectorE: DVE Perf Modes, The perf-mode tier table) puts a tensor_scalar on bf16 data in SBUF in its fastest mode and a float32 tensor_tensor in its slowest. The trace agrees with the order, though the two differ in operation as well as in type.
